# A gated RWKV and feed-forward block on one core: weights turned later, parts of both norms moved to VectorE and GpSimd

## The reference, cut to what matters

```
def layernorm(x): m = mean(x); v = var(x); return (x - m) / sqrt(v + 1e-5)      # over the 256 channels

def birwkv(r, k, v, w, u):            # both directions over the 128 tokens
    ek = exp(k); cur = exp(u + k)
    wkv = (Af + Ab + cur * v) / (Bf + Bb + cur)    # A: decayed sums of ek * v, B: of ek
    return sigmoid(r) * wkv

def ffn(x):                            # fake-quantised activations and weights
    xq = act_fake_quant(x, clip_x)     # the scale comes from max |x| of the whole tensor
    h = act_fake_quant(silu(xq @ Wg.T) * (xq @ Wu.T), clip_down)
    return h @ Wd.T

x = x + tanh(g_xattn) * birwkv(layernorm(x), ctx, ctx, w, u)
x = x + tanh(g_ffn) * ffn(layernorm(x))
```

## Time and profile before

| what | value |
|---|---|
| runs, median (lowest to highest) | 252.05 us (251.74 to 253.44) |
| profiled execution, its own time | 254.3 us |
| its span | 252.6 us |
| mean granted TensorE clock | 0.853 |
| busy: TensorE matmul, VectorE, ScalarE, GpSimd | 68%, 65%, 61%, 39% of the span |
| moved by DMA | 32.16 MB, mean 127 GB/s |

### The profile page before, as it was taken

How to read it: one execution, slowest core, us unless ns; L and a number is a source line. 1 busy time by engine, 2 the same in 40 slices (tenths; PEclk the granted TensorE clock), 3 DMA queues, 4 the chain that set the end, 5 groups by cost and what they waited for, 6 DMA issues and landing times.

```text
span 252.6 us, 3143 instructions
## 1 busy us (share of the span) xinstructions
PE 171.3 (68%) x1030; PEld 122.0 (48%) x1034; DVE 163.7 (65%) x343; ACT 154.6 (61%) x198; POOL 99.4 (39%) x117
## 2 busy tenths in 40 slices
PE   0008876999194795799705475799595994589970
PEld 0003334999193795799704354243232341366640
DVE  0894373255225046088877865359979799899993
ACT  4599962133617246254329996699777794589700
POOL 2586000044022043044367540047354476007992
PEclk9999998999779589799956655599989799689995
DMA  4999979999899069196000000000000000002358
GB/s 125 347 345 349 284 214 247 266 267 288 198 304 263 2 184 282 35 242 176 1 0 3 0 0 0 0 1 4 0 0 0 0 0 0 0 0 86 125 187 271
DMA packets 49279, 32.16 MB, mean 127 GB/s; under 512 B 2289, under 2 KB 49009, under 8 KB 49265
## 3 DMA queue, kind: packets, MB, share of 16 engines
q1 hardware_dynamic: 49120, 31.73, 43.7%
q10 hardware_dynamic: 144, 0.26, 0.3%
HBM read 27.53 MB, written 4.46 MB: 127 GB/s over the span
## 4 chain that ended last, share of the span: by engine, by line
PE 46%; ACT 29%; DVE 13%; POOL 4%; issue 3%; DMA 2%; DVEq 1%; SPq 0%; POOLq 0%
PE ps L798 23%; PE ps L872 10%; ACT z_t L399 8%; PE ps L906 7%; ACT hidden L418 5%; ACT z_t L425 3%; ACT w_int L433 2%; POOL hidden L360 2%; PE ps L785 2%; DVE h_peaks L714 2%; DVE h_space L748 2%; DMA x_all<-in_x 2%; ACT w_intb L441 2%; DVE hidden L703 2%; PE ps L821 2%
## 5 line engine op out<-in xcount | busy, mean ns | idle before, releaser
L798 PE MATMUL ps<-hidden 128*128 128x128 f32 (+1 forms) x512 | 64.9, 295 | 2.5 <-DVE hidden L551 2.5
L798 PEld LDWEIGHTS ps<-hidden 128*128 128x128 f32 x512 | 64.6, 211 | 3.3 <-issue 3.3
L343 POOL TENSOR_TENSOR x_all<-x_all,silu_out 128x512 f32<-128x512 f32 x16 | 24.4, 1526 | 80.8 <-DVE silu_out L613 80.8
L604 DVE SCALAR_TENSOR_TENSOR h_space<-z_t,ps 128x256 f32<-128x256 f32 x32 | 13.4, 418 | 46.1 <-PE ps L798 46.0
L407 ACT ACTIVATE up_out<-h_space 128x512 f32<-128x512 f32 x16 | 10.1, 630 | 47.9 <-DVE h_space L604 47.9
L785 PE MATMUL ps<-hidden,flip 128*128 128x512 f32 x32 | 17.0, 686 | 22.1 <-DMA hidden<-in_ctx 19.7
L872 PE MATMUL ps<-xq,wuT 128*128 128x512 bf16 (+1 forms) x96 | 26.0, 416 | 6.3 <-DVE hidden L703 6.3
L872 PE MATMUL ps<-xq,wgT 128*128 128x512 bf16 (+1 forms) x92 | 25.7, 420 | 3.5 <-ACT xq L501 3.2
L906 PE MATMUL ps<-wdT,z_t 128*128 128x256 bf16 (+1 forms) x192 | 25.4, 288 | 2.6 <-ACT z_t L535 2.6
L714 DVE TENSOR_REDUCE h_peaks<-hidden (+2 forms) x24 | 26.1, 1121 | 0.4
L821 PE MATMUL ps<-ident,hidden 128*128 128x128 f32 x64 | 14.5, 400 | 16.7 <-ACT hidden L418 16.7
(11 more groups left out here) (82 smaller groups left out, 258.7 us busy)
## 6 DMA issues: line engine op xcount, KB each, us to landing
hidden<-lag_w SPq DMA_DIRECT2D x32, 512.0 KB, 5.2
x_all<-in_x SPq DMA_DIRECT2D x8, 512.0 KB, 8.1
hidden<-in_ctx SPq DMA_DIRECT2D x8, 512.0 KB, 9.2
out<-x_all SPq DMA_DIRECT2D x16, 256.0 KB, 2.1
xq<-in_L_ffn_w_down SPq DMA_DIRECT2D x1, 704.0 KB, 4.2
xq<-in_L_ffn_w_gate SPq DMA_DIRECT2D x1, 640.0 KB, 6.4
h_space<-in_L_ffn_w_up SPq DMA_DIRECT2D x1, 640.0 KB, 5.8
lag_w<-silu_out ACTq DMA_DIRECT2D x1, 255.0 KB, 7.2
```

The costliest lines, as they stand in the source:

```text
L343: nc.gpsimd.tensor_tensor(xs, xs, mixed[:, m % 2, :, :].rearrange("p c b -> p b c"), ALU.add).then_inc(s["x1_done"], 1)
L798: last = nc.tensor.matmul(ps[:, j % BANKS, c * 2 * SEQS:end * 2 * SEQS], lag_tile(j)[:, c, :], ekp[:, (j * CK + c) * 2 * SEQS:(j * CK + en ...
```

## The change

Three things are changed. First, TensorE turns the weights behind chunks 14, 21 and 27 instead of 10, 14 and 20; ScalarE casts the second and third behind pairs 8 and 11 (before: 6 and 9) and stores behind pairs 8, 11 and 14 (before: 6, 8 and 11); VectorE's `weight_scales` move to pairs 3, 6 and 9. The weights' loads stay where they were. Second, for groups 0, 2, 4 and 6 the first norm is applied on VectorE (`normalise1`, four tensor_scalar per group, behind the statistics of the next group) and ScalarE takes one exponential of the whole group. Third, in the second norm GpSimd applies one sequence of each group (`normalise_last`), ScalarE the other three; GpSimd computes the scales of group g + 1 ahead of that.

```diff
+        DVE_Z = 0, 2, 4, 6
+        z1 = late[:, 0:2 * GC].rearrange("p (s n) -> p s n", s=2)
+        lag_w = up_out[:, 512:512 + CG * LAGS].rearrange("p (i j) -> p i j", i=CG)
...
+            def normalise_last(g):
+                n = g * GS + GS - 1
+                pool.wait_ge(s["sc2_done"], g + 1)
+                nc.gpsimd.tensor_scalar(z_all[:, n * C:(n + 1) * C], x_all[:, n * C:(n + 1) * C], rs2[:, n:n + 1],
+                                        mr2[:, n:n + 1], ALU.mult, ALU.add).then_inc(s["z_last"], 1)
+            rstd2(0)
             for g in range(GROUPS):
-                rstd2(g)
+                if g + 1 < GROUPS:
+                    rstd2(g + 1)
+                normalise_last(g)
...
             def exp_z(g):
+                if g in DVE_Z:
+                    act.wait_ge(s["z1_done"], DVE_Z.index(g) + 1)
+                    nc.scalar.activation(ez[:, :, g * GS:(g + 1) * GS],
+                                         z1[:, DVE_Z.index(g) % 2, :].rearrange("p (b c) -> p c b", c=C),
+                                         ACT.Exp).then_inc(s["ez_done"], 1)
+                    return
...
-                for i in range(GS):
+                for i in range(GS - 1):
                     n = g * GS + i
                     last = nc.scalar.activation(z_all[:, n * C:(n + 1) * C], xs[:, i, :], ACT.Identity,
...
-                if m == 6:
+                if m == 8:
                     keep_weights(0)
                     quantise_weights(1)
                     cast_weights(1)
-                if m == 8:
+                if m == 11:
                     keep_weights(1)
-                if m == 9:
                     quantise_weights(2)
                     cast_weights(2)
-                if m == 11:
+                if m == 14:
                     keep_weights(2)
...
+            def normalise1(g):
+                i = DVE_Z.index(g)
+                dve.wait_ge(s["sc1_done"], g + 1)
+                wait(dve, s["ez_done"], DVE_Z[i - 2] + 1 if i >= 2 else 0)
+                for k in range(GS):
+                    n = g * GS + k
+                    last = nc.vector.tensor_scalar(z1[:, i % 2, k * C:(k + 1) * C], x_all[:, n * C:(n + 1) * C],
+                                                   nr1[:, n:n + 1], mr1[:, n:n + 1], ALU.mult, ALU.add)
+                last.then_inc(s["z1_done"], 1)
...
             for g in range(GROUPS):
                 stats1(g)
+                if g - 1 in DVE_Z:
+                    normalise1(g - 1)
...
-                if m == 5:
+                if m == 6:
                     weight_scales(1)
-                if m == 8:
+                if m == 9:
                     weight_scales(2)
-                if m == 9:
                     dve.wait_ge(s["ident_set"], 2)
                     down_diagonals()
...
             def turn_z(g):
                 pe.wait_ge(s["z_done"], g + 1)
+                pe.wait_ge(s["z_last"], g + 1)
...
-                if j == 10:
-                    turn_weights(0)
-                if j == 14:
-                    turn_weights(1)
-                if j == 20:
-                    turn_weights(2)
+                if j in (14, 21, 27):
+                    turn_weights((14, 21, 27).index(j))
```

More of the change, by code:

```diff
@@ L117, in gated_rwkv_ffn @@
         lnd = up_out[:, 0:512]
-        lag_w = late[:, 0:CG * LAGS].rearrange("p (i j) -> p i j", i=CG)
+        DVE_Z = 0, 2, 4, 6
+        z1 = late[:, 0:2 * GC].rearrange("p (s n) -> p s n", s=2)
+        lag_w = up_out[:, 512:512 + CG * LAGS].rearrange("p (i j) -> p i j", i=CG)
         lag_row = down_row[:, :, :].rearrange("p j c -> p (j c)")[:, 0:LAGS]
@@ L194, in gated_rwkv_ffn @@
             "ctx_back", "ek_done", "pk_done", "ab_done", "den_done", "ln_done", "rden_done", "mix_done", "x1_done",
-            "bn1_done", "mv1_done", "ve1_done", "rs1_done", "sc1_done", "ez_done",
-            "bn2_done", "mv2_done", "ve2_done", "rs2_done", "sc2_done", "z_done", "zT", "z_kept", "peak_done",
+            "bn1_done", "mv1_done", "ve1_done", "rs1_done", "sc1_done", "z1_done", "ez_done",
+            "bn2_done", "mv2_done", "ve2_done", "rs2_done", "sc2_done", "z_done", "z_last", "zT", "z_kept", "peak_done",
             "top_done", "topT",
@@ L618, in peak_z @@
                 dve.wait_ge(s["z_done"], g + 1)
+                dve.wait_ge(s["z_last"], g + 1)
                 nc.vector.tensor_reduce(peaks[:, g:g + 1], z_all[:, g * GC:(g + 1) * GC], AX.X, ALU.max,
@@ L665, in _ @@
             assert done == SEQS
-            late_stats(0)
-            late_stats(1)
-            for g in range(2, GROUPS):
+            for g in range(GROUPS):
+                if g >= 3:
+                    peak_z(g - 3)
                 late_stats(g)
-                peak_z(g - 2)
-            peak_z(GROUPS - 2)
-            peak_z(GROUPS - 1)
+            for g in range(GROUPS - 3, GROUPS):
+                peak_z(g)
             def global_peak(tile, prefix, quotient, scale, inverse):
```

## The result

| what | before | after |
|---|---|---|
| runs, median (lowest to highest) | 252.75 us (251.74 to 253.89) | 235.75 us (232.88 to 237.91) |
| profiled execution, its span | 252.6 us | 234.8 us |
| its own time | 254.3 us | 236.88 us |

The ratio is 0.925, 95% interval 0.915 to 0.935: the change takes 7.5% off the time. It compares the fast executions of both kernels alone (all four before, 232.88 and 234.61 us after), so it is not the quotient of the medians, 0.933. The forecast was 230.2 us with a range of 226.5 to 236.5. For the profiled execution it was 232.2 us, and that took 236.9: the direction and the place are right, the gain is 4.7 us smaller than the sum.

A forecast was written before the change was run, and what follows sets the result against it. The bounding chain ran through ScalarE's exponentials, TensorE's chunks with 15.0 us waiting for casts, the second norm and feed-forward. Gains 0.6 + 18.8 + 2.7 = 22.1 us took 254.3 to 232.2, as a median 230.2; range 226.5 to 236.5.

The forecast's parts named there:

- The turns: Chunk stage: later turns end TensorE's waits for casts, 83.2 us become 64.4, a gain of 18.8 (13.3 to 21.8).
- the wait for chunk 15's load: Chunk stage: TensorE waits 2.0 us for chunk 15's data, queued behind the third weight; bounds 0.5 and 3.3 us.
- the wait for the third cast: Chunk stage, third turn: 1.0 us of waiting, between 0 and 2, because VectorE is late with the reciprocals.
- the loads rival: Chunk 15 waits 3.3 us or more, the clock falls, later loads trail TensorE; some 5 us more, 235 us; chance 0.15.
- The first norm: Before the first chunk: half the norm on VectorE gains 0.6 us, not ScalarE's 5.8, as VectorE becomes late.
- the exponential's price: First norm: ScalarE's whole-group 128x1024 exponential, priced like `exp_k` at 0.85 to 0.95 us, replaces 2.4 us per group.
- The port: Rival, first norm: `normalise1` waits behind GpSimd's small operations, 4.4 us more, median 234.5 us; chance 0.25.
- The second norm: Last residual to last emptied bank: a quarter on GpSimd cuts the period from 2.87 to 2.4 us, gaining 2.7.
- The late start: Second norm: the third normalisation starts 8.7 instead of 8.4 us after the last residual, as emptying waits for GpSimd; costs 0.3.
- GpSimd as the bound of the second norm: Rival, second norm: GpSimd's new operation takes about 1.07 us and the gain is nil; 233 us, chance 0.12.
- the casts did not end TensorE's waits: Rival, chunk stage: TensorE still stands before each turn as long as now, only the second-norm gain remains; 249 us, chance 0.03.
- the clock did not stay low through the chunks: Rival, chunk stage: short waits keep TensorE's clock at 0.5, 1.64 us more per chunk; 258 us with 17, chance 0.02.

The follow-up runs named there:

- The first part alone: The kernel before with only the later turns and the new places of casts, stores and `weight_scales`; ratio 0.935 (0.927 to 0.943).
- the channel-major kernel: The changed kernel with up and down weights' loads moved and VectorE writing the normalised group channel by channel; ratio 0.915 (0.906 to 0.923).
- the run with one scalar: The changed kernel with the shift by the mean left out of VectorE's four first-norm operations; 347 instead of 407 ns each, first chunk at 41.46 us.

## Why the prediction was right, and where its sum was off

**The turns.** The step held: the three waits for casts were on the path, and nothing of their size took their place. The first part alone gives 0.935. Sum 64.4 us for the chunk stage, measured 65.6. Of its terms, the wait for chunk 15's load was 3.0 us instead of 2.0 (within the stated 0.5 to 3.3; a landing of 6.1 us instead of the median 5.2), the wait for the third cast 0 in the changed kernel and 0.4 alone (1.0 forecast), and the turns are 0.67 us each between their neighbours instead of 0.84. A term was missing: the three small loads in SyncE's queue before chunk 21's load, 1.08 us. They stood in the queue of the kernel before too, behind chunk 20's load; the prediction wrote that nothing more is lost behind chunk 15. They cost a wait in two of the seven profiles that have the loads in these places (1.08 and 0.61 us). These terms make 65.0; the last 0.6 us is spread over the breaks between the runs of chunks. Where nothing waits for loads, the stage takes 61.75 us with a slow first chunk, and the sum has 61.4 for that. The tail from the last chunk to the last residual is 4.4 us, as forecast 4.3.

**The clock.** The sum takes the first chunk at the low clock, "as now", and the wait before chunk 15 at the high one. Both came out so in the changed kernel's profile, and neither is a property of the kernel. The first chunk took 2.9 to 3.6 us in six of the 14 profiles and 2.1 in eight, always behind 2.46 us of idle time. The wait before chunk 15 stands in seven profiles. The clock stayed at 1.00 behind 2.40, 3.00 and 3.24 us of it; it fell to 0.50 behind 2.60, 2.69, 2.77 and 2.99 us, and the seven chunks behind it took 1.6 to 3.0 us more than 12.5. So the loads rival's condition, that the clock falls there, was met in four of seven, at waits shorter than its 3.3 us, and that it was not met in the profile of the changed kernel is luck.

**The first norm.** This is the step that failed, in sign: 0.6 us gained was forecast, 0.6 us later is measured, and 0.9 us against the kernels without it (41.25 and 41.17 us). The chain that ended last shows the path:

```profile
20.33 1.07 DVE silu_out L601 x3
21.42 1.98 ACT z_t L410
...
26.74 1.90 ACT z_t L410
```

VectorE is late up to group 4, as the prediction has it, and from there ScalarE is. The term that was mis-sized is the exponential's price. It was taken from `exp_k`, which reads from PSUM and writes runs of 16 bytes: 0.95 us against 1.96. Because group 4's took so long, ScalarE came to group 6's 0.3 us after VectorE had finished (26.64 against 26.32 us), and then needed 0.9 us more for it. VectorE itself was on time: its operations cost 1.30 us per group instead of 1.08, but the statistics ahead of them 1.73 to 1.77 instead of 1.93 start to start, and `normalise1(6)` ended 19.9 us after the first statistics began, for 19.8 in the forecast. With the exponential at 1.06 us (the channel-major kernel) the first chunk starts at 41.06 us, near the forecast's 40.9, and near the 41.27 of the kernel without the part on the same chip. The part as it could have been is worth 0.2 us.

**The port.** As a rival it had 0.25. Its mechanism is real and measured, its condition was not met: the small operations did not hold VectorE up for as long as they last. It did not happen.

**The second norm.** 2.2 us gained for 2.7. By its own terms the forecast was 2.85 - 0.3 = 2.55; the 2.7 is a slip. The late start (8.7 us to the third normalisation) and the shorter last period (0.5) came as forecast. The rest is the period: two of the five are 2.6 us and not 2.4, 0.4 us together. Two things make them longer. GpSimd's operation is 0.56 us for 0.5 and, in every other group, GpSimd waits 0.30 us for VectorE's statistics. And TensorE's transposition of 1.95 us lies between GpSimd and ScalarE:

```profile
122.90 1.95 PE ps L852 x8
124.88 1.02 ACT z_t L444
```

The sum has no price for it. TensorE's granted clock is 0.50 from 117 to 129 us here. In the run with one scalar the same transposition ran in 1.07 us, and the period there was 2.37 us with GpSimd's operation unchanged; its whole stage took 24.8 us. That the clock is all of the difference was not tried by itself.

**The rest.** The feed-forward's 1.3 us are no effect of the change: the same code took 92.0 to 93.9 us in eight of the other profiles and 97.0 to 97.2 in four, without regard to what was changed ahead of it. Its stretches show where the two lengths differ. In the changed kernel, 40 to 50 and 60 to 70 us into the stage:

```profile
177.80:187.80 10.00, 10.00 (x40) 3.84 (x39) 7.50 (x8) 6.95 (x8) 6.03 (x3) 0.77 0.00 0
...
197.80:207.80 10.00, 8.14 (x44) 6.17 (x45) 9.31 (x15) 7.32 (x7) 0.00 (x0) 0.57 0.00 0
```

and in the kernel with the down weights' load moved, at the same distances:

```profile
173.70:183.70 10.00, 9.82 (x49) 4.12 (x48) 9.61 (x10) 8.92 (x10) 7.38 (x4) 1.00 0.00 0
...
193.70:203.70 10.00, 9.44 (x71) 7.33 (x70) 9.89 (x12) 9.35 (x8) 0.03 (x1) 0.80 0.00 0
```

The longer one has the lower granted clock there, and fewer matmuls in the same time. That the clock makes the whole difference was not tried. Of the other rivals, GpSimd as the bound of the second norm shows a part of at most 0.4 us; the casts did not end TensorE's waits, and the clock did not stay low through the chunks.

The measured 235.75 us lies 0.75 us inside the range, and 5.5 us from the forecast. The upper end of the range stood for the port and for late loads with a fallen clock. Neither happened in the profile; four smaller misses in one direction, the feed-forward's among them, filled the same room. That they stayed inside it is partly luck.

## What to carry to other kernels

When an in-order engine waits for work that another engine does once, move the waiting instruction behind work that is ready, and then look through every queue for what was hidden by the old wait: here the transfers' queue, with a weight's load and three loads of a few bytes ahead of the data, became late next. Compare stages only between executions in which the clock did the same, or count its share apart: here it moved a stage by 1.3 to 5 us with no edit near it. Moving work from a busy engine to a less busy one pays only to the point where the second becomes late, and the price of the moved step must come from a row with the same memory and the same step between elements, not only the same size. Where an effect is smaller than the spread of the totals, read it from the stage's boundaries in the profile.

## What the runs showed of the hardware that was not expected

A ScalarE activation on 128x1024 float32 takes 1.06 us when it reads SBUF in one run and writes in one run or in runs of 16 bytes, and 1.94 to 1.99 us when one side goes element by element with steps of 128 bytes or 1 KB. VectorE's tensor_scalar, writing one float32 every 16 bytes, took 1.49 instead of 1.38 us for four. VectorE's tensor_scalar waited out a GpSimd product of 1.89 us whole, and showed no delay beyond 5 ns beside GpSimd operations on 128x4, even one of 1.05 us; GpSimd's add took 0.30 to 0.34 instead of 0.20 us there. The idle stretches of 4.5 to 5.3 us in the kernel before were followed by a granted clock of 0.50. Shorter ones were not all alike: 2.46 us before the first chunk and 2.60 to 2.99 us before chunk 15 were followed by 0.50 in some executions, and 2.40, 2.46, 3.00 and 3.24 us by 1.00 in others, so their length alone does not say which.
